# Edge table ranked by column quarters, split aggregation groups and an earlier set-up of the last stage in a gated graph layer on one core

## What is computed

```python
h = relu(layernorm(x))
u = h @ root + bias
for r in range(8):            # mean over the edges of type r that end in a node
    mask = (edge_type == r)
    sums = segment_sum(h[src] * mask[:, None], dst, num_segments=1250)
    cnt = segment_sum(mask, dst, num_segments=1250)
    u = u + (sums / maximum(cnt, 1.0)[:, None]) @ weight[r]
z = concatenate([u, h], axis=1) @ w_gate + b_gate
out = x + tanh(u) * z + h * (1.0 - z)
```

## Time and profile before

| | us |
|---|---|
| median of 3 runs | 1519.31 |
| lowest, highest | 1516.27, 1519.83 |
| the profiled execution, its own time | 1518.65 |
| its span in the trace | 1516.9 |
| TensorE busy | 1311.0 (86%) |
| VectorE busy | 939.5 (62%) |
| GpSimd busy | 732.7 (48%) |
| ScalarE busy | 408.9 (27%) |

### The profile page before, as it was taken

How to read it: one execution, slowest core, us unless ns; L and a number is a source line. 1 busy time by engine, 2 the same in 40 slices (tenths; PEclk the granted TensorE clock), 3 DMA queues, 4 the chain that set the end, 5 groups by cost and what they waited for, 6 DMA issues and landing times.

```text
span 1516.9 us, 20122 instructions
## 1 busy us (share of the span) xinstructions
PE 1311.0 (86%) x6165; PEld 655.7 (43%) x6165; DVE 939.5 (62%) x1328; ACT 408.9 (27%) x501; POOL 732.7 (48%) x994
## 2 busy tenths in 40 slices
PE   3979997999998498988887999997887789977798
PEld 1434443444443244444443444443443344434465
DVE  6677686476656355753555667665544557684776
ACT  5442231232324113221222143232201213433000
POOL 2412007787878566665635547543656465320000
PEclk9999998999999799999998999999999989989899
DMA  5632141252234277766754774774676857664886
GB/s 204 212 135 78 53 158 37 49 165 51 62 107 133 76 231 244 218 176 218 221 160 139 264 225 147 254 229 128 191 244 201 273 166 212 225 197 134 212 221 185
DMA packets 108104, 259.15 MB, mean 171 GB/s; under 512 B 20826, under 2 KB 21329, under 8 KB 108020
## 3 DMA queue, kind: packets, MB, share of 16 engines
q1 hardware_dynamic: 75204, 175.63, 35.7%
q0 software_dynamic: 32816, 82.39, 19.6%
HBM read 194.34 MB, written 82.17 MB: 182 GB/s over the span
## 4 chain that ended last, share of the span: by engine, by line
PE 27%; DMA 24%; POOL 19%; issue 13%; DVE 10%; ACT 3%; SPq 2%; POOLq 1%; DVEq 0%; ACTq 0%
PE ps L1272 22%; DMA early<-y_rows,idx 18%; POOL table_rows L571 15%; PE ps L1233 5%; DMA out_dram<-hT 3%; POOL onehot L605 2%; DVE W L900 2%; DMA y_rows<-yhl 1%; POOL early L597 1%; DMA hT<-u_rows 1%; DVE hT L948 1%; DVE hT L953 1%; POOL dcol L586 1%; ACT early L689 1%; DMA W<-in_L_gnn_weight_dram 1%
## 5 line engine op out<-in xcount | busy, mean ns | idle before, releaser
L1272 PE MATMUL ps<-W,hT 128*128 128x512 f16 (+2 forms) x4860 | 1100.9, 387 | 24.4 <-DVE W L900 23.3
L1272 PEld LDWEIGHTS ps<-W,hT 128*128 128x128 f16 (+2 forms) x4860 | 499.7, 104 | 581.5 <-issue 52.4
L1233 PE MATMUL ps<-early,onehot 128*125 x768 | 208.4, 409 | 107.4 <-POOL onehot L605 97.3
L571 POOL DMA_INDIRECT table_rows<-edge_src,table_i x160 | 225.9, 1412 | 146.2 <-DVE table_i L973 89.4
L597 POOL DMA_INDIRECT early<-y_rows,idx x192 | 222.7, 1160 | 118.0 <-PE ps L1236 70.3
L605 POOL TENSOR_SCALAR onehot<-iota_d,dcol 128x125 f16<-128x125 f16 x184 | 153.2, 833 | 210.7 <-DMA early<-y_rows,idx 207.2
L729 ACT ACTIVATE yhl<-W 128x512 f16<-128x512 f32 x120 | 75.3, 628 | 444.3 <-DVE W L1024 242.3
L1233 PEld LDWEIGHTS ps<-early,onehot 128*125 x768 | 103.8, 143 | 173.7 <-issue 130.3
L900 DVE SCALAR_TENSOR_TENSOR W<-W,wsc 128x2048 f16<-128x2048 f32 x65 | 153.2, 2361 | 25.9 <-ACT W L679 21.0
L679 ACT ACTIVATE W<-W,wsc 128x2048 f16<-128x2048 f32 x65 | 128.2, 1989 | 16.9 <-DVE W L916 11.8
L648 ACT ACTIVATE peek_out<-W 128x1024 bf16<-128x1024 f32 x84 | 88.4, 1052 | 95.6 <-DMA W<-in_L_gnn_weight_dram 74.7
(11 more groups left out here) (162 smaller groups left out, 715.4 us busy)
## 6 DMA issues: line engine op xcount, KB each, us to landing
y_rows<-yhl SPq DMA_DIRECT2D x144, 256.0 KB
W<-in_L_gnn_weight_dram SPq DMA_DIRECT2D x32, 1024.0 KB
early<-u_rows SPq DMA_DIRECT2D x40, 448.0 KB
u_rows<-early SPq DMA_DIRECT2D x40, 448.0 KB
W<-in_L_gnn_w_gate_dram SPq DMA_DIRECT2D x8, 1024.0 KB
early<-in_x_dram SPq DMA_DIRECT2D x9, 512.0 KB, 4.4
hs_rows<-early SPq DMA_DIRECT2D x9, 512.0 KB, 2.9
u_rows<-yhl SPq DMA_DIRECT2D x18, 256.0 KB
```

The source lines that it names most:

```text
L571: pool.indirect_dma_start(out=table_rows, out_offset=bass.IndirectOffsetOnAxis(ap=at_i[:, c:c + 1], axis=0), in_=packed[0:EP, c:c + 1], in ...
L1233: nc.tensor.matmul(ps[0:DT, 4 + half, :], hot_t, rows[:, bass.ds(ring_slot * (2 * D) + (half * D + part * HC), HC)], start=first and part ...
L1272: last = nc.tensor.matmul(ps[0:rows, n % 4, :], hT[:, m, v_h, k, n0:n0 + rows], Wh[:, MAT[w][c], v_w, k, :], start=(first and v_h + v_w == ...
```

## The change

Five edits, made together.

1. **Ranks by column quarters.** rank and RANK_AT are gone. positions(b) now first adds the group starts to the counts and multiplies by the mask, two operations over 80 groups x 40 columns, and then reduces. It runs at units 21, 25, 29 and 33.
2. **One copy of table columns.** edge_src and edge_dst become one tensor, edges, with the two values side by side; idx and dcol become pair. columns makes one copy of two elements.
3. **Split groups.** sum_group becomes sum_first, after unit AGG_AT[g], and sum_rest, after unit REST_AT[g], one unit later where the next group is two or more units away (not in the third sweep, nor for the last group). STEP_END, and with it store_u, load_u, row_scale and turn_u, follow REST_AT. The first sweep's AGG_AT begins at 98 in place of 102 and ends at 162 as before; table() moves with it from 99 to 95.
4. **Scale matmul later.** weight_max two units after weight_top in place of one, weight_scale three after in place of two (of one for gate_u).
5. **gate_u and last stage.** Conversions at -5, -4, -3, -2 before unit 305 in place of -5, -3, -2, -1, each in the slot that the one before has left, and so each waiting for it; the low parts follow one unit later. The first four units are (0, left), (1, left), (0, right), (1, right). h, x and tanh(u) of the first tiles are loaded from unit 301 on; after gate_h's last store only zh of tiles 0 and 1 and the rest of tile 2 are.

```diff
+    ORDER_U = [(0, 0), (1, 0), (0, 1), (1, 1)] + [(j, h) for j in range(2, NJ) for h in range(2)]
...
-    AGG_AT = ([102 + g * 63 // 30 for g in range(30)] + [168 + g * 68 // 20 for g in range(20)]
+    AGG_AT = ([98 + g * 67 // 30 for g in range(30)] + [168 + g * 68 // 20 for g in range(20)]
...
-    AGG = {}
+
+    REST_AT = [AGG_AT[g] + (1 if g + 1 < NG and AGG_AT[g + 1] >= AGG_AT[g] + 2 and group(g)[0] != 2 else 0) for g in range(NG)]
+    AGG, REST = {}, {}
     for g in range(NG):
         AGG.setdefault(AGG_AT[g], []).append(g)
+        REST.setdefault(REST_AT[g], []).append(g)
     STEPS = [(s, j) for s in range(NS) for j in range(NJ)]
-    STEP_END = [AGG_AT[SPAN[s][0] + (j + 1) * (SWEEPS[s][1] - SWEEPS[s][0]) - 1] for s, j in STEPS]
+    STEP_END = [REST_AT[SPAN[s][0] + (j + 1) * (SWEEPS[s][1] - SWEEPS[s][0]) - 1] for s, j in STEPS]
...
-    RANK_AT = {21 + i: range(10 * i, 10 * i + 10) for i in range(8)}
-    POSITIONS_AT = {29 + i: i for i in range(SQ)}
+    POSITIONS_AT = {21: 0, 25: 1, 29: 2, 33: 3}
...
-    MAT[W_GU] = [MAT[W_GU][0], MAT[W_GU][1], LAND[W_GU][0], LAND[W_GU][1]]
+    MAT[W_GU] = [MAT[W_GU][0]] + LAND[W_GU][0:3]
...
-    CONV_AT = {0: [], 1: [17, 18, 22, 24], 2: [35, 36, 42, 44], W_GU: [FIRST[W_GU] + d for d in (-5, -3, -2, -1)]}
+    CONV_AT = {0: [], 1: [17, 18, 22, 24], 2: [35, 36, 42, 44], W_GU: [FIRST[W_GU] + d for d in (-5, -4, -3, -2)]}
...
-    SCALE_AT[W_GU] = FIRST[W_GH] + 27
+
+    SCALE_AT[W_GU] = next(n for n in range(FIRST[W_GH] + 26, FIRST[W_GU]) if n + 1 not in TURN_U and n + 2 not in TURN_U)
...
+        edges = sb("edges", [P, TMAX, 2], I32)
...
+        pair = sb("pair", [P, RING, 2], I32)
...
+        key, packed = eflat[:, 0:EC].bitcast(F32), eflat[:, EC:2 * EC]
+        idx, dcol = pair[:, :, 0:1], pair[:, :, 1:2].bitcast(F32)
...
-        zh_in, h_in, x_in, t_in = ([fin[NZ * v + b] for b in range(NZ)] for v in range(4))
+        zh_in, h_in, x_in, t_in = ([fin[i] for i in at] for at in ((5, 6, 9), (0, 2, 4), (1, 3, 7), (10, 11, 8)))
...
+            def load_part(j, part):
+                b = j % NZ
+                to, of = {"zh": (zh_in, zh_rows), "h": (h_in, hs_rows), "x": (x_in, x), "t": (t_in, u_rows)}[part]
+                if part == "t":
+                    k = FINAL + j
+                    sp.wait_ge(s[f"u_stored{k % 3}"], 32 * (k // 3 + 1))
+                for n0, p0, rows in halves(*DTL[j]):
+                    sp.dma_start(to[b][p0:p0 + rows, :], of[n0:n0 + rows, :]).then_inc(s[f"z_loaded{b}"], 16)
...
-            def load_z(j):
-                b = j % NZ
-                sp.wait_ge(s[f"u_stored{k % 3}"], 32 * (k // 3 + 1))
...
+                if n == FIRST[W_GU] - 4:
+                    sp.wait_ge(s["gemm_done"], phase_end(W_GH, 5))
+                    for b in range(2):
+                        sp.wait_ge(s[f"hs_stored{b}"], 16 * NJ // 2)
+                    for j, part in ((0, "h"), (0, "x"), (1, "h"), (1, "x"), (2, "h")):
+                        load_part(j, part)
+                    sp.wait_ge(s[YDONE], out_no(unit(W_GH, 5, HT - 1)) + 1)
+                    load_part(0, "t")
+                if n == FIRST[W_GU] - 2:
+                    load_part(1, "t")
...
-            for j in range(NZ):
-                load_z(j)
+            for j, part in ((0, "zh"), (1, "zh"), (2, "x"), (2, "t"), (2, "zh")):
+                load_part(j, part)
             for j in range(NJ - 1):
-                store_out(j, 2 * j + 2, slice(0, D))
+                store_out(j, max(i for i in range(2 * NJ) if ORDER_U[i][0] == j) + 1, slice(0, D))
...
-                    load_z(j + NZ)
+                    for part in ("h", "x", "t", "zh"):
+                        load_part(j + NZ, part)
...
-                pool.tensor_copy(dcol[:, b, :], edge_dst[:, bass.ds(t, 1)]).then_inc(s["idx_ready"], 1)
-                pool.tensor_copy(idx[:, b, :], edge_src[:, bass.ds(t, 1)]).then_inc(s["idx_ready"], 1)
+                pool.tensor_copy(pair[:, b, :], eflat[:, bass.ds(t * 2, 2)]).then_inc(s["idx_ready"], 1)
...
+                elif w == W_GU and c:
+                    act.wait_ge(s["w_lo"], conv_no(w, c - 1) + 1)
...
-            def rank(groups_of):
...
+                q = slice(b * EC // SQ, (b + 1) * EC // SQ)
                 dve.wait_ge(s["scan_ready"], SQ)
-                for g in groups_of:
-                    nc.vector.scalar_tensor_tensor(out=pos3[:, g, :], in0=scan3[:, g, :], scalar=tb[0:EP, g:g + 1],
-                                                   in1=hot3[:, g, :], op0=ALU.add, op1=ALU.mult).then_inc(s["ranked"], 1)
...
-                dve.wait_ge(s["ranked"], NG)
                 dve.wait_ge(s["table_filled"], 16)
+                step(nc.vector.tensor_tensor(pos3[:, :, q], scan3[:, :, q], tb[0:EP, :].unsqueeze(2).to_broadcast([EP, NG, EC // SQ]),
+                                             ALU.add))
+                step(nc.vector.tensor_tensor(pos3[:, :, q], pos3[:, :, q], hot3[:, :, q], ALU.mult))
                 step(nc.vector.tensor_reduce(pos[:, q], pos3[:, :, q].rearrange("p g c -> p c g"), AX.X, ALU.add))
...
+                step(nc.vector.tensor_scalar(edges[:, :, 0], table_i[:, :], 7, None, ALU.logical_shift_right))
...
-                nc.vector.tensor_copy(edge_dst[:, :], table_i[:, :]).then_inc(s["table_ready"], 1)
+                nc.vector.tensor_copy(edges[:, :, 1].bitcast(F32), table_i[:, :]).then_inc(s["table_ready"], 1)
...
-                j, half = divmod(n - FIRST[W_GU], 2)
+                j, half = ORDER_U[n - FIRST[W_GU]]
...
-                for g in AGG.get(n - 1, ()):
+                for g in REST.get(n - 1, ()):
                     add_group(g)
...
-                    if (n - FIRST[W_GU]) % 2 == 0:
-                        prepare_tile((n - FIRST[W_GU]) // 2)
+                    if ORDER_U[n - FIRST[W_GU]][1] == 0:
+                        prepare_tile(ORDER_U[n - FIRST[W_GU]][0])
...
-                if n in RANK_AT:
-                    rank(RANK_AT[n])
...
-                if n - (2 if n < FIRST[W_GH] else 1) in TOPS:
-                    weight_scale(TOPS[n - (2 if n < FIRST[W_GH] else 1)])
+                if n - 3 in TOPS:
+                    weight_scale(TOPS[n - 3])
...
-            def sum_group(g):
+            def sum_first(g):
                 t0 = pe.value_load(bounds[0:1, g:g + 1], min_val=0, max_val=TMAX - RING)
-                t1 = pe.value_load(bounds[0:1, g + 1:g + 2], min_val=2, max_val=TMAX)
                 if g:
                     pe.wait_ge(s["u_added"], g)
                 else:
                     pe.wait_ge(s["table_ready"], 1)
                 sum_tile(t0, True)
+
+            def sum_rest(g):
+                t0 = pe.value_load(bounds[0:1, g:g + 1], min_val=0, max_val=TMAX - RING)
+                t1 = pe.value_load(bounds[0:1, g + 1:g + 2], min_val=2, max_val=TMAX)
                 with pe.Fori(t0 + 1, t1) as t:
                     sum_tile(t, False)
...
-                if n - 1 in TOPS:
-                    weight_max(TOPS[n - 1])
+                if n - 2 in TOPS:
+                    weight_max(TOPS[n - 2])
...
-                for g in AGG.get(n, ()):
-                    sum_group(g)
+                for g in range(NG):
+                    if AGG_AT[g] == n:
+                        sum_first(g)
+                    if REST_AT[g] == n:
+                        sum_rest(g)
```

24 lines of the change are left out of this document (5 added, 19 removed).

## The result

The changed kernel takes **1473.58 us** (median of 4 runs, 1469.74 to 1480.54) against 1519.41 (4 runs): a ratio of **0.9711**, 95% interval 0.9682 to 0.9740. That is 45.8 us less; about 40 were forecast. The profiled execution took 1475.66 us with a span of 1473.8, against 1516.9 before.

The account below looks back on a forecast made before the run. TensorE is busiest, but the sorted table starts the first sweep and GpSimd's ring of gathers paces it. Terms 20 + 4.7 + 7.2 + 3 + 4 - 4 + 4 = 38.9 off 1518.65 gave 1479 us, range 1461 to 1497.

Parts of the forecast that it names:

- The price of the new operations: Table: each new VectorE operation of the ranks by quarters takes 3.5 us, with bounds 3.48 and 6.82.
- The scatters' loss: Table: new operations and two conversions hold scatters back 17.6 us, some 3 us regained; net table about 20 us earlier.
- The copy's 4.6 us: First sweep: one table copy less saves 0.13 us in each of 35 rounds, 4.6 us; 3 us in the third.
- the four units: First sweep: four more units, 11 us, fit its holes; 251 us of busy time against 264 of supply.
- the split: First sweep: one unit runs in the wait for a group's later tiles, 2.6 us at the last hole only.
- bound by TensorE: Sign that the forecast is wrong: the first sweep turns out bound by TensorE, not by the ring of gathers.
- The holes for wspread: After the table wait: a later scale matmul gains 2.7 of a 3.07 us hole and 2.10 of another, 4.7 us.
- The order of stores: Ends of sweeps: u store and reload come behind the last y store, 2 us at each of two, 4 us.
- Rival D: Split makes TensorE wait for VectorE's sum; at 0.8 us for each of 59 groups 1526 us; chance 0.04.
- only four loads stand in that queue: Last stage: zh load comes some 6 us later, but behind four loads, not 24, so tile 0's loads stay at 1403.84.
- Rivals A and C: A: last stage pays in full, 1467 us, chance 0.15. C: new operations take 6.82 us, 1506 us, chance 0.10.
- B: Scatters hardly held, 8 us less lost; ring gains 6 more from the missing copy; 1465 us, chance 0.14.

Follow-up runs that it names:

- e2: Changed kernel with the mask multiplication done twice in quarters 1 to 3; one run, first to last scatter 306.2 us, first tile at 515.69 us.
- e1: Changed kernel with the ranks made as before, ten operations in each of units 21 to 28; 1494.74 us, ratio 0.9823 to the kernel before.
- e8: Changed kernel with two one-element copies for each tile again; 1482.13 us, ratio 0.9761 to the kernel before.
- e5: Changed kernel with the first sweep's groups starting at unit 102 instead of 98; 1473.04 us, ratio 0.9685 to the kernel before.
- e6: Changed kernel without the split, each group's rest summed right behind its first tile; 1495.18 us, ratio 0.9824 to the kernel before.
- e9: The changed kernel run once more, unaltered, beside three other follow-up kernels on their chip; 1483.33 us, ratio 0.9762 to the kernel before.
- e10: Changed kernel with the last sweep's groups summed in one piece, ends of steps kept; 1480.03 us, ratio 0.9730 to the kernel before.
- e3: Changed kernel with the whole last stage as before: conversions, order of units and loads; 1483.67 us, ratio 0.9741 to the kernel before.
- e4: Changed kernel without the early loads, the last stage's conversions and unit order kept; 1483.05 us, ratio 0.9749 to the kernel before.
- e7: Changed kernel with the scale matmul one unit after weight_top again; 1489.68 us (three runs), ratio 0.9821 to the kernel before.
- e12: Changed kernel with last sweep in one piece, output stores on ScalarE's queue and first sweep from unit 102; 1471.84 us, ratio 0.9681 to the kernel before.
- e11: Changed kernel with output tiles 0 to 8 stored from ScalarE's DMA queue; 1470.30 us, ratio 0.9663 to the kernel before.

## Why the prediction was right, point by point

*The table.* Forecast 34.3 us for the first scatter, measured 36.2, of which 1.9 stood already at unit 20. The price of the new operations, 3.5, was right. The scatters' loss was put at 17.6 - 3 = 14.6 us and is 16.1; by e2 each operation costs 2.8, not 2.5, and by e1 (279.0 us) the two terms are 18.8 and 2.6. The 2.6 us between the last scatter and the first tile I had not seen: the table moved onto a place where weight quadrants are summed. 17.5 of 20.

*The first sweep.* Here two terms were wrong, and the gain was 3.3 us (2.2 by the average of nine), less than half of the 7.2. The copy's 4.6 us do not exist (e8): in its trace the copies' time is taken from GpSimd's waits for TensorE. The step that failed was "a gather goes out once the gather two before it has landed, so 35 rounds x 0.13": in e8 the landings' waits didn't move. That the four units go into the holes for nothing failed by some 5 us (e5): busy time below supply as a sum doesn't mean that each unit finds a hole. What made up for both in part was the split, put at 2.6 us and worth 8 by e6, 4 to 5 of it at an equal clock: it was charged with one hole only, while it acts at many of the 14 waits for a one-hot that e6 shows, of which the earlier trace rows is the last of before. The sweep's last sum was to end near 764 and ended at 773.4 (780.4 in e9; 791.6 before). The sign "bound by TensorE" showed in part: four units less are 5 us less, and the length follows TensorE's clock.

*The second sweep.* 6.7 forecast, 10.3 and (e9) 7.5 measured. The holes for wspread gave 5.2 us (3.07 and 2.10) in the changed profile against 4.7 forecast, and 3.5 in e9, where 1.66 were left. The order of stores was put at 2 us for each sweep's start; TensorE's first hole fell from 8.15 to 5.23 us at the second sweep and from 7.63 to 3.11 at the third, 2.9 and 4.5.

*The third sweep.* 5 forecast, 3 of them by the copy, which e8 denies; 6.2 measured, with 4.5 from TensorE's first hole, so more than the store order's 2. Executions of the same code lie 10 us apart here, so the rest can't be split up.

*The last sweep.* 4 us of loss forecast, 1.2 measured. Rival D's mechanism is real (waits for the sum went from 3 to 13, from 5.3 to 23.9 us), but most of these waits stand where another wait would have stood, so it never came near a loss: in the first sweep they replace waits for gathers, in the last e10 shows waits for ScalarE behind them.

*The last stage.* The argument held: the end hangs on loads and on SyncE's rounds, not on TensorE's hole. 4 us forecast; 7.0 and 5.5 measured against before, 5.4 and 3.9 by e3. Its inner steps hold too, counted from unit 302: tile 0 prepared at 22.1 us, as before (22.3), the first store 1.1 us sooner (1 forecast), the second 4.9 (3.5 forecast), the rounds 11.3 us in place of 11.6. e4 shows both sides of "only four loads stand in that queue": without the early loads tile 0 comes 2.6 us later than before, not 6. One sign of being wrong did show: by the forecast's own count, unit 305 to the end, the stage shrank by 10.8 us (11.8 in e9), more than 10. That is because 3.9 us (6.4 in e9) moved ahead of unit 305, among them the 3.7 us wait for ScalarE; the whole stretch gained 7.0.

*The sum.* 38.9 forecast, 43.1 in the first profile and 36.1 in e9's. The forecast's own range of 1468 to 1490 holds both medians, 1473.58 and 1483.33. The waits were read rightly at the table, in the second sweep and in the last stage. That the total fits so well is in part luck: the copy's 7.6 us and the 5 us of the four units were missing, and the split, the shorter holes at the sweeps' starts and TensorE's busy time, 7 to 16 us less and in no term, stood in for them. Rivals A and C fell (the last stage did not pay 16 us, though TensorE's end came 14.8 us sooner in it; the new operations take 3.5 us). B's first half fell with e2, its second with e8.

What stays open: why the granted clock of the first sweep and the hole behind unit 193 differ between executions of the same code, what spreads the third sweep over 10 us, and hence how much of e1's 14 to 16 us reaches the end.

## What to carry to other kernels

Ask of a hole what ends the stage, not how long the hole is: closing the longest hole of the last stage (16.33 us) gained nothing while the loads came late (e4), and moving one kind of DMA to another queue, where no hole stood, was worth 10 us. A saved instruction on an engine that waits for others saves nothing: it waits longer (e8). Before a single profile is compared with another, compare TensorE's busy time for the same matmuls in the stretch, since it alone moved the first sweep by 7 us and more. And where an edit puts a new wait in the place of an old one, add up both before calling it a cost: 12.7 us of new waits came with 8 us of gain.

## What the runs showed of the hardware

A short hole of TensorE can cost more than its length. In e1 a hole of 1.85 us behind unit 193 is followed by 24 matmuls that take 7.03 us, where they take 5.34 without a hole; the stretch from unit 192 to 200 grew by 3.5 us for 1.85 (30.1 against 26.6). The granted clock was 1.00 in the hole, and 0.50 from 891.4 to 893.4 us, behind it.

```profile
889.43 0.49 PE L1228 MATMUL ps<-ident,wspread 128*128 128x128 f32 x2 [1.85 <-DVE wspread L893]
889.75 7.03 PE L1290 MATMUL ps<-W,hT 128*128 128x512 f16 x24
```

After e7's hole of 5.13 us the granted clock was 0.50, that is the lower level, 1.2 GHz of 2.4, in the four microseconds behind it, and four matmuls took 1.94 us where they take 1.03. Units 192 to 200 took 34.8 us there, 8.2 more for 5.13. But length alone doesn't decide. Holes of 1.15, 1.66 and 1.73 us behind unit 193 (e12, e9, e5) lengthen the same stretch by 1.2 to 1.8 us, about their own length, while those of 1.85 to 2.55 (e1, e8, e10, e2, e11) lengthen it by 3.5 to 4.3; and in the kernel before, the hole of 3.07 us at 899.34 is followed by 36 matmuls in 7.93 us, which is the fast pace.

Where a VectorE operation of the table reads two tensors in SBUF (3.48 and 3.49 us), it holds GpSimd's scatter until it has ended, and the scatter ends 1.06 us after it; the reduction, which reads one, doesn't (1.19 us). An operation of 3.49 us costs the chain of scatters 2.8 us (e2).
